# A fused two-layer transformer kernel: the rows of split minima are sent to the stacked buffers from ScalarE's queue in place of SP's

## The reference

```python
attn = jnp.einsum('bhqd,bhkd->bhqk', q, k) * scale
...
attn = jnp.where(allowed, attn, -jnp.inf)
attn = jax.nn.softmax(attn, axis=-1)
...
scores = jnp.einsum('bqhd,bkhd->bhqk', q, k) / math.sqrt(hd)
...
probs = jax.nn.softmax(scores, axis=-1)
```

## Time and profile before

| | |
|---|---|
| median of 2 runs | 1819.33 us (1819.02 to 1819.64) |
| the profiled execution | 1819.52 us, of which 1817.4 us are its span |
| instructions | 36028 |
| PE busy | 1693.4 us, 93% |
| DVE busy | 1216.3 us, 67% |
| ACT busy | 926.3 us, 51% |
| POOL busy | 871.7 us, 48% |
| mean granted PE clock | 0.974 |

### The profile page before, as it was taken

The page is one execution under the profiler, slowest core; times in us unless marked ns, Lnnn a source line. Parts: engine busy times, 40 slices in busy tenths (PEclk is TensorE's granted clock), DMA queues, the critical chain, the costliest instruction groups (busy, mean ns, idle before and its releaser), DMA issues.

```text
span 1817.4 us, 36028 instructions
## 1 busy us (share of the span) xinstructions
PE 1693.4 (93%) x12015; PEld 1124.9 (62%) x12015; DVE 1216.3 (67%) x2638; ACT 926.3 (51%) x1961; POOL 871.7 (48%) x1323
## 2 busy tenths in 40 slices
PE   7899998999999999999999999999869999999990
PEld 5666765665567656555765655554456777777770
DVE  4557677868657787774779767788447666666504
ACT  2455463656665355566555656666623444333323
POOL 3674664532458674234858524337352433333233
PEclk9999999999999899999999999999989999999995
DMA  4925247042154403205540412341221433333126
GB/s 134 178 72 70 37 107 141 4 69 78 41 78 78 93 14 52 61 32 72 95 72 6 53 43 56 41 96 27 72 94 61 93 90 90 90 90 67 22 29 196
DMA packets 106065, 131.40 MB, mean 72 GB/s; under 512 B 15882, under 2 KB 77467, under 8 KB 105744
## 3 DMA queue, kind: packets, MB, share of 16 engines
q1 hardware_dynamic: 91552, 117.70, 30.4%
q0 software_dynamic: 14336, 11.41, 4.6%
HBM read 53.96 MB, written 38.01 MB: 51 GB/s over the span
## 4 chain that ended last, share of the span: by engine, by line
PE 68%; DVE 11%; issue 5%; DMA 4%; ACT 4%; POOL 4%; SPq 1%; DVEq 0%; POOLq 0%; ACTq 0%
PE b_psum L1789 19%; PE b_psum L734 8%; PE b_psum L1009 8%; PE b_psum L995 7%; PE b_psum L948 7%; PE b_psum L982 6%; DMA before_last_norm<-b_ye,b_ids 3%; DVE b_mneg L1398 2%; PE b_psum L745 2%; DVE b_mhalf L1398 2%; PE b_psum L975 2%; ACT b_probs L1134 2%; PE b_psum L740 2%; PE b_psum L978 1%; PE b_psum L1017 1%
## 5 line engine op out<-in xcount | busy, mean ns | idle before, releaser
L1134 ACT ACTIVATE b_probs<-b_psum 128x512 f32<-128x512 f32 (+3 forms) x896 | 417.8, 544 | 182.9 <-PE b_psum L995 181.2
L1398 DVE TENSOR_REDUCE b_mneg<-b_psum 128x2 f32<-128x384 f32 (+5 forms) x608 | 332.0, 591 | 85.7 <-PE b_psum L982 84.6
L1497 POOL TENSOR_SCALAR_AFFINE_SELECT b_probs<-b_probs 128x512 f32<-128x512 f32 (+1 forms) x400 | 240.0, 612 | 285.5 <-ACT b_probs L1134 274.8
L982 PE MATMUL b_psum<-b_qk 96*128 96x192 bf16 (+4 forms) x1280 | 293.4, 295 | 3.2 <-DVE b_mneg L1398 1.1
L995 PE MATMUL b_psum<-b_qk 99*128 99x192 bf16 (+5 forms) x1344 | 262.6, 290 | 10.8 <-DMA b_qk<-b_mrow 5.3
L1743 POOL DMA_INDIRECT before_last_norm<-b_ye,b_ids x64 | 102.1, 1596 | 274.0 <-DMA before_last_norm<-b_ye,b_ids 152.1
L1009 PE MATMUL b_psum<-b_probs,b_v 128*32 128x192 f32 (+4 forms) x2688 | 198.0, 415 | 3.9 <-POOL b_probs L1497 3.0
L982 PEld LDWEIGHTS b_psum<-b_qk 96*128 96x128 bf16 x1280 | 123.4, 99 | 94.5 <-issue 25.8
L1398 DVE TENSOR_REDUCE b_mhalf<-b_psum 128x1 f32<-128x512 f32 x256 | 165.0, 680 | 14.7 <-PE b_psum L982 14.3
L1513 POOL TENSOR_TENSOR b_rot<-b_product 128x128 f32<-128x128 f32 x256 | 113.3, 476 | 124.8 <-PE b_psum L967 53.8
L995 PEld LDWEIGHTS b_psum<-b_qk 99*128 99x128 bf16 x1344 | 113.2, 98 | 91.9 <-issue 22.3
(11 more groups left out here) (289 smaller groups left out, 3301.3 us busy)
## 6 DMA issues: line engine op xcount, KB each, us to landing
b_qk<-b_split SPq DMA_DIRECT2D x372, 128.0 KB, 5.3
slot_rows<-before_last_norm SPq DMA_DIRECT2D x32, 256.0 KB, 3.8
b_qk<-in_W SPq DMA_DIRECT2D x8, 1024.0 KB, 7.3
b_xg<-slot_rows SPq DMA_DIRECT2D x16, 512.0 KB, 9.5
b_w<-in_W SPq DMA_DIRECT2D x8, 1024.0 KB, 7.9
before_last_norm<-b_early SPq DMA_DIRECT2D x4, 1024.0 KB, 4.4
b_o<-before_last_norm SPq DMA_DIRECT2D x4, 1024.0 KB, 6.0
before_last_norm<-b_o SPq DMA_DIRECT2D x4, 1024.0 KB, 4.5
```

The costliest lines, as they stand in the source:

```text
L982: ins = pe.matmul(out[:, i, :], q[0:KS, h, P * t:P * t + P], q[0:KS, HG + h, a:e], start=not last, stop=True, skip_group_check=True)
L1134: act.activation(probs_of((g, h2, t), a, e)[:, heads[0]:heads[-1] + 1, :], bank, ACT.Exp, scale=SCALE).then_inc(s.exp_done, 1)
L1398: dve.tensor_reduce(out, in_bank(("max",) + x[1:], heads, e - a), AX.X, ALU.max, negate=True).then_inc(s.max_read, 1)
L1497: ins = pool.affine_select(out=block, in_=block, pattern=[[0, HG], [1 if ahead else -1, z - y]], compare_op=ALU.is_ge, fill=none, base=y - ...
```

## The change

The step `spread` moves from SP to ACT. Its planned cost becomes 0.7 in place of 0.5. In the code its branch leaves SP's loop and enters ACT's, with the same wait (`rows_read`, which the copy of the same unit raises), source, destination and semaphore. The wait now stands on ACT itself, before the DMA. As the planner's lists depend on engines and costs, all lists may come out in another order.

```diff
-            add(("spread", g, h), "SP", 0.5, ("lines", g, h))
+            add(("spread", g, h), "ACT", 0.7, ("lines", g, h))
...
-                elif kind == "spread":
-                    _, g, h = x
-                    n = unit_number(g, h)
-                    sp.wait_ge(s.rows_read, n + 1)
-                    sp.dma_start(u.qk[g % RING][KS:KS + 3, 0:HG, BANK * h:BANK * h + BANK], u.mrow[n % 2][0:3 * HG, :]
-                                 ).then_inc(rows_sent[n % 2], 16)
...
+                elif kind == "spread":
+                    _, g, h = x
+                    n = unit_number(g, h)
+                    act.wait_ge(s.rows_read, n + 1)
+                    act.dma_start(u.qk[g % RING][KS:KS + 3, 0:HG, BANK * h:BANK * h + BANK], u.mrow[n % 2][0:3 * HG, :]
+                                 ).then_inc(rows_sent[n % 2], 16)
```

## The result

The kernel after takes 1872.0 us (1868.5 to 1875.5, 2 runs) where the one before took 1819.3: ratio 1.029, 95% interval 1.0256 to 1.0323. It is slower, and outside the predicted range. Timed again twice, it took 1871.1 and 1862.1 us (ratios 1.0279 and 1.0262).

A forecast was written before the change was run, and what follows sets the result against it. It took PE, busy 93% of the span, as the bound. To the profiled 1819.5 us it added 5.1 for ACT and subtracted 3.5 and 0.5, giving 1820.6, rounded 1821; range 1805 to 1839.

The forecast's parts named there:

- What is removed: On SP, 64 issues and 64 waiting points go, so later loads start earlier: gain 0.5 us, bounds 0 and 4.
- Landing: Spreads on ACT's queue no longer stand behind SP's earlier issues and land sooner: gain 3.5 us, bounds 0 and 5.3.
- The tail: Last unit's spread, 5.61 us to land behind four transfers of experts' weights and biases; expected gain 2.5 us.
- Rival 4: Transfers share DMA engines, the last spread keeps its 5.61 us, the 3.5 gain goes: 1824 us; no separate chance.
- the early crowd of loads: Start of the kernel, where the other late spreads were placed, as at 74.79 straight after 14 loads.
- What ACT gets: ACT takes a wait, an issue and collisions per unit, 64 us in all, of which 5.1 reach the end.
- The 5.1 us charged: Part of ACT's added 64 us expected to reach the end, by its 8% chain share; bounds 0 and 64.
- Rival 1: ACT's held queue delays exponentials after the copy and PE stops at its banks: 1840 to 1866 us; chance 0.20.
- The order: Replanned instruction orders, bank numbers and fillers on all engines: taken as 0, with 10 us either side.
- the prediction's signs of being wrong: An issue costing ACT much more than SP, or the new order moving PE's idle time by over 15 us.

The follow-up runs named there:

- experiment 3: Kernel after, spread still issued by ACT, but SP waits for the copy at each spread's planned place, issuing nothing: 1824.9 us, ratio 1.0028.
- experiment 9: Kernel after, but from the fourth group on each load moves only half of its columns: 1820.8 us, ratio 1.0005.
- experiment 6: Kernel before, but ACT also waits for each copy and issues a small transfer nobody reads; spread stays on SP: 1820.7 us, ratio 1.0014.
- experiment 1: Kernel before with its instruction lists unchanged, except that ACT issues the spread right behind its copy: 1858.7 us, ratio 1.021.
- experiment 5: Kernel after, unchanged, timed again beside other runs: 1871.1 us, ratio 1.0279.
- experiment 2: Kernel after with its instruction lists, but SP issues the spread at its planned place: 1818.0 us, ratio 0.9989.
- experiment 13: Kernel after, with filler products ahead of PE's wait for the rows in the twelve units where it stood longest: 1855.3 us, ratio 1.0214.
- experiment 8: Kernel before, with the first expert's weights issued behind the last spread in SP's list: 1813.7 us, ratio 0.9968.

## Why the prediction was wrong

- **The step that failed is "What is removed".** It saw that the 64 points at which SP stands before later work fall away, and that 19 loads were ready behind one of them, and booked this as a gain of 0.5 us with bounds 0 and 4. It had no bound on the side of a loss. The cost of loads that start earlier wasn't asked: they stand before the next spread. Experiments 3 and 9 show this effect as nearly the whole of the loss, 47 of 53 us and all of it; the prediction had no rival for it. SP's 554 us of waits were read as "SP's queue delays nothing"; they were also what kept the loads back.
- **"Landing" had the wrong sign.** Expected was a gain of 3.5 us, bounds 0 and 5.3; measured, PE's waits for the rows rose by 34.2 us. The bound "at worst nothing gets earlier" took the loads' moments from before as fixed, while the other edit moved them. The rule of the Trainium skill cited there (DMA: Bandwidth & Descriptors, "Issuing engines are not separate DMA queues": all issuers share the 16 DMA engines) agrees with the trace: a spread from ACT, issued at 501.39, landed at 508.79 beside the load issued next to it. The tail too: the chain of after has

```profile
1332.34 5.17 DMA b_qk<-b_mrow
```

  in place of 5.61. ACT does have a queue of its own (q10), and at 937.03 the spread passed two of the five loads that had not landed, one of them still being issued; at 78.35, the worst unit, and at 501.39 it passed none. Rival 4 had this mechanism, but only for the tail, at 3.5 us. One reading of the trace of before was wrong as well: apart from the tail, PE's waits for the rows do not lie in the early crowd of loads but at 292, 498 and 574 us, 2.0 us together.
- **"What ACT gets" held, in after's lists.** The issue took 0.73 us (forecast 0.84 with its overhead), started 0.03 us after the copy, and PE's waits for ACT went from 12.7 to 13.7 us in the attention part. The charge of a held engine for every unit was too high in one way: in 25 of the 64 units the new list has an exponential between copy and issue, as at 501.26 above, and ACT computes while the copy ends and the issue runs. The 5.1 us charged are, if anything, too much for after (experiments 6 and 9); with the old lists up to 8.5 us may be due to it (experiment 1). Rival 1, the only one far on the slow side, gave 1840 to 1866 us for a reason that is not what costs the time here; that the measured time lies just above its end is chance, and doesn't bear it out.
- **"The order"** was taken as 0, give or take 10. With SP's stop kept, 1818.0 us confirms it; without it the order adds some 9 to 15 us (experiments 1 and 5). PE's idle time did move by over 15 us, one of the prediction's signs of being wrong, but not by the order: in experiment 2 it is 123.1 us, in before 124.0.
- **A third part was not foreseen**: after a wait PE's products are slower. Of the 49.4 us of span, 34.2 are waits for the rows, and PE's busy time is up by 17.3, without the fillers by 24.0. The new order can have only a smaller part in that: the same lists with the spread on SP (experiment 2) are up by 8.5 in the execution profiled (1696.6 - 28.7 against 1659.4), at a mean clock of 0.969. Experiment 13 makes the clock the cause as far as busy time and mean clock tell (0.958 to 0.969); the gain in time itself, 6.7 us, isn't clear of its intervals.

What stays open: when a transfer on a queue of its own passes those issued before it on the other (by 0.3 us at 937.03, not at all at 501.39), why the new order loses more than the old one when the loads run free, and how much of the gain of experiment 8 is the last wait.

## What to carry to other kernels

A queue that stands idle at a wait may be the thing that holds other transfers back: before a small urgent transfer is taken out of a queue of large ones, ask what the queue then sends in its place, and whether those bytes are ahead of the next urgent one. Compare the pace of issue (here 0.67 us) with the pace of landing (1.08 us): where issues are faster a pile grows, and what is issued behind it lands late, here whichever engine issued it. And what must land last need not be issued first: the first expert's weights behind the last spread gave 0.3% (0.2 to 0.5).

## What the hardware showed that was not expected

- A transfer of 12 rows of 1 KB from ACT's queue took 7.40 us when nine loads of 128 KB had been issued before it from SP's queue, of which six had not landed yet; it landed with its neighbours by time of issue. Another, issued at 937.03 with five loads not yet landed, took 3.83 us and landed before two of them, one of which was still being issued.
- With PE waiting for the rows 16 times, up to 6.4 us each, its mean granted clock is 0.958 where it was 0.974. The clock has two levels in these traces, full (1.00, 2.4 GHz) and half (0.50, 1.2 GHz); so these means stand for some 157 us at half in after ((1 - 0.958) x 2 x 1866.8) and some 94 in before. The columns are as in the earlier trace rows. Of the two stretches of after, the first holds the wait of 6.4 us and the second has no wait for the rows; before has 0.97 in the first:

```profile
50.00:100.00 50.00, 37.75 (x354) 25.75 (x352) 21.62 (x44) 19.15 (x49) 31.10 (x62) 0.83 1.00 205
...
800.00:850.00 50.00, 48.78 (x342) 25.58 (x334) 27.71 (x50) 35.60 (x77) 18.13 (x36) 1.00 0.27 39
```

  Closer up, the end of that wait and the products behind it, both at half clock:

```profile
84.00:89.00 5.00, 0.00 (x0) 0.00 (x0) 0.00 (x0) 0.00 (x0) 0.00 (x0) 0.50 1.07 137
89.00:95.00 6.00, 5.77 (x46) 4.28 (x47) 0.92 (x3) 4.03 (x11) 4.20 (x8) 0.50 1.09 318
```

- An issue on ACT of twelve rows took 0.73 us for rows of 1 KB into three partitions of four blocks (L1157), and 0.30 us for rows of 768 B into contiguous rows in DRAM (experiment 6).
